# The second routing done batch by batch inside the last attention's loop, with fixed slots per expert

## What is computed

```python
x = x + xattn0(layernorm(x), ctx, ...)      # 16 heads of 32, causal
x = x + ffn0(layernorm(x), ...)             # 8 experts, top 2, gelu, 512 -> 2048 -> 512
x = x + xattn1(layernorm(x), ctx, ...)      # 16 heads of 64; keys and values: own rows and 722 context rows
x = x + ffn1(layernorm(x), ...)             # 8 experts, top 2, silu(gate)*up, 512 -> 1024 -> 512

# ffn1:
logits = einsum('bsd,ed->bse', x, w_router)
top_vals, top_idx = top_k(logits, 2); rw = softmax(top_vals)
h = silu(x @ w_gate[e].T) * (x @ w_up[e].T); y = h @ w_down[e].T   # for the two experts of each row
out = layernorm(sum(rw * y of the chosen experts)) * ln_gamma + ln_beta
```

## Time and profile before

| | us |
|---|---|
| median of 3 runs | 1887.82 |
| profiled execution | 1884.81 |
| its span, first to last instruction | 1883.2 |
| TensorE busy | 1651.2 (88%) |
| VectorE busy | 1075.2 (57%) |
| ScalarE busy | 769.7 (41%) |
| POOL busy | 135.2 (7%) |

### The profile page before, as it was taken

One profiled execution on the slowest core, in us unless ns is written; L12 is line 12 of the kernel. 1 busy time (PEld: TensorE's weight loads), 2 busy tenths in 40 slices (PEclk: granted clock), 3 DMA queues, 4 the chain that ended last, 5 costly groups with the idle time before them and its releaser, 6 DMA issues. The chain is left out here.

```text
span 1883.2 us, 31881 instructions
## 1 busy us (share of the span) xinstructions
PE 1651.2 (88%) x11680; PEld 1399.7 (74%) x11680; DVE 1075.2 (57%) x1776; ACT 769.7 (41%) x1464; POOL 135.2 (7%) x177
## 2 busy tenths in 40 slices
PE   6997359999999779989999899899998619999993
PEld 5785349999999469668787687678777519999981
DVE  5775547677666552246556365456555327767765
ACT  2453135555555232235444254435444015445440
POOL 4000320000000300200000000000000040000004
PEclk9998569999999889989999899999999659999997
DMA  9300165665566434231110101111000065555634
GB/s 345 138 9 1 60 235 203 204 212 206 200 204 210 130 132 148 86 119 33 31 44 23 46 17 46 34 30 41 22 17 9 1 226 197 207 210 192 218 135 125
DMA packets 83938, 223.51 MB, mean 119 GB/s; under 512 B 32904, under 2 KB 39432, under 8 KB 68748
## 3 DMA queue, kind: packets, MB, share of 16 engines
q1 hardware_dynamic: 68412, 175.72, 28.0%
q0 software_dynamic: 15440, 46.56, 7.1%
HBM read 180.61 MB, written 41.62 MB: 118 GB/s over the span
## 5 line engine op out<-in xcount | busy, mean ns | idle before, releaser
L955 DVE TENSOR_TENSOR e_lo<-e_raw,e_hi 128x2048 fp32r<-128x2048 f32 x118 | 270.4, 2291 | 129.0 <-ACT e_hi L1018 129.0
L918 PE MATMUL banks<-e_xh,e_hi 128*128 128x256 f32 x1024 | 292.1, 285 | 12.3 <-DVE e_xl L971 7.4
L1564 PE MATMUL banks<-a_ch,a_wm 128*128 128x362 f32 (+1 forms) x1024 | 286.0, 341 | 10.4 <-DVE a_cl L1680 10.4
L918 PE MATMUL banks<-e_xl,e_hi 128*128 128x256 f32 x1024 | 291.4, 285 | 0.0
L918 PE MATMUL banks<-e_xh,e_lo 128*128 128x256 f32 x1024 | 291.4, 285 | 0.0
L1018 ACT CAST e_hi<-e_raw 128x2048 fp32r<-128x2048 f32 x118 | 224.7, 1904 | 70.5 <-PE banks L935 28.6
L918 PEld LDWEIGHTS banks<-e_xh,e_hi 128*128 128x128 f32 x1024 | 197.6, 193 | 20.7 <-issue 8.2
L918 PEld LDWEIGHTS banks<-e_xl,e_hi 128*128 128x128 f32 x1024 | 197.7, 193 | 5.6
L918 PEld LDWEIGHTS banks<-e_xh,e_lo 128*128 128x128 f32 x1024 | 197.6, 193 | 0.0
L1564 PEld LDWEIGHTS banks<-a_ch,a_wm 128*128 128x128 f32 x1024 | 186.6, 191 | 12.3 <-DVE a_cl L1680 11.8
L1693 DVE TENSOR_REDUCE a_nmax<-banks 100x1 f32<-100x822 f32 x128 | 123.5, 1006 | 107.8 <-PE banks L1598 107.8
(11 more groups left out here) (236 smaller groups left out, 2690.7 us busy)
## 6 DMA issues: line engine op xcount, KB each, us to landing
e_raw<-wout SPq DMA_DIRECT2D x50, 1024.0 KB, 4.8
e_raw<-w SPq DMA_DIRECT2D x34, 1024.0 KB
e_raw<-wgate SPq DMA_DIRECT2D x17, 1024.0 KB
e_raw<-wup SPq DMA_DIRECT2D x17, 1024.0 KB, 4.9
a_craw<-ctxT SPq DMA_DIRECT2D x32, 361.0 KB, 3.8
e_xs<-slot_rows SPq DMA_DIRECT2D x18, 512.0 KB
slot_outs<-e_y POOLq DMA_DIRECT2D x16, 512.0 KB, 3.2
slot_rows<-a_zero POOLq DMA_DIRECT2D x15, 512.0 KB, 10.4
```

The source lines that it names most:

```text
L918: mm = nc.tensor.matmul(ps[:, bank, 0:CAP], w[:, cc, cut], x[:, cc, :], start=t == 0, stop=t == len(terms) - 1)
L955: nc.vector.tensor_tensor(lo[g % 2][i][:], raw[q % RAW][:], hi[g % 2][i][:].bitcast(F32), ALU.subtract)\
L1564: mm = nc.tensor.matmul(ps[:, 6 + half, 0:wide], w[:, cc, cut], x[:, cc, start:start + wide], start=cc == 0 and t == 0, stop=cc == DC - 1 ...
```

## The change

- The loop over batches of the last attention is written out: eight batches in a row, no hardware loop.
- Routing 1 has no stage of its own. In each batch the batch before is routed: output in pair 1 (now ahead of the value product), statistics and root in pair 2, rows in pair 3, turn in 4, logits and best expert in 5, second expert in 6, ranks and slot in 7, then two scatters on POOL's queue. The last batch is routed after the loop.
- Each expert has 1024 fixed slots (`SPAN`), so a slot needs only the count so far. A second table `first_row` gives each pass its first slot. The slot buffer for rows is larger (33 x 256 rows in place of 15), with more zeroing at the start; the results of layer 1 have a buffer of their own (8192 rows), which is first filled by four copies of 4 MB inside device memory on POOL's queue, after the scatters of batches 0 to 3.
- During the last batch SP loads three weight chunks of the first expert; two are split in high and low parts into the space of the context weights. It is always expert 0, as each expert now has a pass at least.
- The softmax of the two chosen logits moves to the start of combine 1.
- Turned probabilities have two buffers in place of four, the attention's output one in place of two.

```diff
+SPAN = CAP * -(-B * T // CAP)
...
-        self.rows = nc.dram_tensor("slot_rows", ((PASSES + 1) * CAP, D), F32, kind="Internal").ap()
-        self.outs = nc.dram_tensor("slot_outs", (PASSES * CAP, D), F32, kind="Internal").ap()
+        self.first_row = self.sb(ctx, "first_row", [1, 16], I32)
+        self.best = self.sb(ctx, "best", [T, 2, B])
+        self.rows = nc.dram_tensor("slot_rows", (E * SPAN + CAP, D), F32, kind="Internal").ap()
+        self.outs0 = nc.dram_tensor("slot_outs0", (PASSES * CAP, D), F32, kind="Internal").ap()
+        self.outs1 = nc.dram_tensor("slot_outs1", (E * SPAN, D), F32, kind="Internal").ap()
...
-                for t, n in ((k.rows, PASSES + 1), (k.outs, PASSES)):
+                pool.wait_ge(w_in["o"], 16)
+                for t, n in ((k.rows, E * SPAN // CAP + 1), (k.outs0, PASSES)):
                     for r in range(n):
                         pool.dma_start(t[CAP * r:CAP * (r + 1)].rearrange("(p s) d -> p (s d)", p=128),
                                        zero[:]).then_inc(zeroed, 16)
-                pool.wait_ge(zeroed, 16 * (2 * PASSES + 1))
+                pool.wait_ge(zeroed, 16 * (E * SPAN // CAP + 1 + PASSES))
...
-        raw = [k.sb(c, f"{L}raw{q}", [128, 4, 512]) for q in range(RAW)]
-        hi = [[k.sb(c, f"{L}hi{u}_{n}", [128, 4, 512], F32R) for n in range(CH)] for u in range(2)]
-        lo = [[k.sb(c, f"{L}lo{u}_{n}", [128, 4, 512], F32R) for n in range(CH)] for u in range(2)]
...
+        READY = 0 if ahead1 is None else len(ahead1.hi)
+        raw = [k.sb(c, f"{L}raw{q}", [128, 4, 512]) for q in range(RAW)] if ahead1 is None else ahead1.raw
...
-                n = sp.value_load(last, min_val=LEAST, max_val=PASSES)
+                if ahead1 is not None:
+                    for q in range(CH):
+                        sp.sem_inc(w_in[q], 16)
...
+                def first_row(j):
+                    if ahead1 is None:
+                        return j * CAP
+                    if type(j) is int:
+                        return 0
+                    return sp.value_load(k.first_row[0:1, bass.ds(j, 1)], min_val=0, max_val=E * SPAN)
...
-                first = expert(0)
-                load(0, first, FIRST)
-                sp.wait_ge(scattered, 16 * 2 * B)
-                rows(0)
-                load(0, first, LATE)
+                if ahead1 is None:
+                    n = sp.value_load(last, min_val=LEAST, max_val=PASSES)
+                    first = expert(0)
+                    load(0, first, FIRST)
+                    sp.wait_ge(scattered, 16 * 2 * B)
+                    rows(0)
+                    load(0, first, LATE)
+                else:
+                    rows(0)
+                    n = sp.value_load(last, min_val=LEAST, max_val=PASSES)
...
-                for b in range(B):
+                for b in range(B if ahead1 is None else 0):
...
-                    pool.dma_start(k.outs[bass.ds(j * CAP, CAP), :].rearrange("(s p) d -> p s d", p=128), y[:])\
+                    first = j * CAP if ahead1 is None else \
+                        pool.value_load(k.first_row[0:1, bass.ds(j, 1)], min_val=0, max_val=E * SPAN - CAP)
+                    outs = k.outs0 if ahead1 is None else k.outs1
+                    pool.dma_start(outs[bass.ds(first, CAP), :].rearrange("(s p) d -> p s d", p=128), y[:])\
...
+                    nc.vector.tensor_tensor(sm[:, 0, :], k.best[:, 1, :], k.best[:, 0, :], ALU.subtract).then_inc(dif, 1)
+                    dve.wait_ge(wexp, 1)
+                    own.link(nc.vector.tensor_scalar(sm[:, 1, :], sm[:, 0, :], 1.0, None, ALU.add))
+                    own.link(nc.vector.reciprocal(k.wt[:, 0, :], sm[:, 1, :]))
+                    own.link(nc.vector.tensor_tensor(k.wt[:, 1, :], k.wt[:, 0, :], sm[:, 0, :], ALU.mult))
...
+                    act.wait_ge(dif, 1)
+                    nc.scalar.activation(sm[:, 0, :], sm[:, 0, :], ACT.Exp).then_inc(wexp, 1)
...
+    def __init__(self, k, ctx, s1):
+        self.names = ["wgate", "wup", "wout1"]
+        self.raw = [k.sb(ctx, f"e1_raw{q}", [128, 4, 512]) for q in range(3)]
+        self.hi = [s1.wm[0][:, :, 512 * i:512 * i + 512] for i in range(2)]
+        self.lo = [s1.wm[1][:, :, 512 * i:512 * i + 512] for i in range(2)]
+
...
-    OUTPUT_AT = 1
+    OUTPUT_AT, STATS_AT, ROWS_AT, TURN_AT, LOGITS_AT, SECOND_AT, RANK_AT = 1, 2, 3, 4, 5, 6, 7
...
+    CLEAR = 4
+    CLEAR_ROWS = E * SPAN // CLEAR
...
-        PT = [k.sb(c, f"a1_PT{u}", [128, len(KB1), T]) for u in range(4)]
-        yT = [k.sb(c, f"a1_yT{u}", [128, IC, T]) for u in range(2)]
+        PT = [k.sb(c, f"a1_PT{u}", [128, len(KB1), T]) for u in range(2)]
+        yT = k.sb(c, "a1_yT", [128, IC, T])
...
         def over_steps(eng, step):
 
-            def batch(b, u):
+            for b in range(B):
                 for m in range(IC):
-                    step(b, u, m)
-
-            batch(0, 0)
-            with eng.Fori(0, (B - 2) // 2) as i:
-                batch(2 * i + 1, 1)
-                batch(2 * i + 2, 0)
-            batch(B - 1, 1)
+                    step(b, b % 2, m)
...
+                    if b == B - 1 and m < len(ahead1.raw):
+                        sp.dma_start(ahead1.raw[m][:], a[ahead1.names[m]][0]).then_inc(raw_in[m], 16)
...
+                sp.wait_ge(raw_in[len(ahead1.raw) - 1], 16)
...
+                for b in range(B):
+                    pool.wait_ge(va, b + 1)
+                    pool.tensor_tensor(rs[:, b:b + 1], rs[:, b:b + 1], k.nhalf[:, 0:1], ALU.pow).then_inc(rstd, 1)
+                    pool.wait_ge(slotted, b + 1)
+                    for j in range(2):
+                        pool.indirect_dma_start(out=k.rows[:, :],
+                                                out_offset=bass.IndirectOffsetOnAxis(ap=k.slot[:, j, b:b + 1], axis=0),
+                                                in_=rows[b % 2][:], in_offset=None).then_inc(scattered[b % 2], 16)
+                    if b < CLEAR:
+                        part = slice(CLEAR_ROWS * b, CLEAR_ROWS * (b + 1))
+                        pool.dma_start(k.outs1[part].rearrange("(p s) d -> p (s d)", p=128),
+                                       k.outs0[0:CLEAR_ROWS].rearrange("(p s) d -> p (s d)", p=128))\
+                            .then_inc(cleared, 16)
+                pool.wait_ge(cleared, 16 * CLEAR)
+                for u in range(2):
+                    pool.wait_ge(scattered[u], 16 * B)
...
-                def output(b, u):
+                def keys_copied(b, m):
+
+                    if exists(IC * b + m + 2):
+                        pe.wait_ge(k_v, IC * b + m + 3)
+
+                def output(b):
 
                     pe.wait_ge(ys, IC * (b + 1))
-                    if later(b):
-                        pe.wait_ge(k_v, IC * (b + 1) + OUTPUT_AT + 3)
+                    keys_copied(b + 1, OUTPUT_AT)
...
+
+                def route_turn(b):
+                    pe.wait_ge(rn, b + 1)
+                    keys_copied(b + 1, TURN_AT)
+                    for cc in range(DC):
+                        mm = nc.tensor.transpose(ps[:, 7, T * cc:T * cc + T], rows[b % 2][:, 128 * cc:128 * cc + 128],
+                                                 k.ident[0:T, 0:T])
+                    mm.then_inc(rt, 1)
+
+                def route_logits(b):
+                    pe.wait_ge(rx, b + 1)
+                    if b == 0:
+                        pe.wait_ge(w_in, 16)
+                    keys_copied(b + 1, LOGITS_AT)
+                    for cc in range(DC):
+                        mm = nc.tensor.matmul(ps[0:T, 7, 0:E], rxT[:, cc, :], wg[:, cc, :],
+                                              start=cc == 0, stop=cc == DC - 1)
+                    mm.then_inc(lg, 1)
+
+                def route_rank(b):
+                    pe.wait_ge(sel_r, b + 1)
+                    if b == 0:
+                        pe.wait_ge(made_more, 1)
+                    keys_copied(b + 1, RANK_AT)
+                    nc.tensor.matmul(ps[0:T, 7, 0:E], upper[:], sel[:], start=True, stop=True)
+                    nc.tensor.matmul(ps[0:T, 7, E:2 * E], ones[:], sel[:], start=True, stop=True).then_inc(rk, 1)
...
+                    if m == TURN_AT + 1:
+                        after(pe, rx, b)
+                    if m == LOGITS_AT + 1:
+                        after(pe, lgc, b)
+                    if m == (RANK_AT + 1) % IC:
+                        after(pe, rkc, b - 1)
                     memory_ahead(b, u, m, 1)
                     if exists(p + 1):
                         turn_values(p + 1, (m + 1) % IC)
+                    if m == OUTPUT_AT and b >= 1:
+                        output(b - 1)
                     if prev:
                         attended(p - 1, *back(b, m))
-                    if m == OUTPUT_AT and exists(p - IC):
-                        output(b - 1, 1 - u)
+                    if m == TURN_AT and b >= 1:
+                        route_turn(b - 1)
+                    if m == LOGITS_AT and b >= 1:
```

(95 more changed lines are left out.)

133 lines of the change are left out of this document (114 added, 19 removed).

## The result

Over four runs each, the changed kernel takes 1835.88 us in the median (1834.92 to 1839.31) and the kernel before 1887.53 us. The ratio is 0.9738, with a 95% interval of 0.9726 to 0.9749: 2.6% faster. The forecast was 1833 us, in a range of 1823 to 1852. The profiled execution took 1834.92 us and its span is 1833.3 us, against 1884.81 and 1883.2 before.

A forecast was written before the change was run, and what follows sets the result against it. TensorE was taken as nearly always busy in the last attention and mostly idle from there to the experts. Span 1883.2 - 21.1 + 11.3 - 43.3 = 1830.1, execution 1831.7, median put at 1833 us, range 1823 to 1852.

The forecast's parts named there:

- Part 1: Last attention's loop written out straight: the two loop jumps go, -21.1 us, or 0 if the wait came with the address.
- Part 2: Routing of batches 0 to 6 inside the last attention's loop: 1.6 us per batch on TensorE, +11.3 us, bounds +8 to +28.
- the room of 0.85 us: Pair 5 of the loop: from the end of the turned probabilities' copy to the values' turn; maxima about 0.7 us late.
- -9.8: Forecast shift in us of the last statistics at the attention's end, against 1478.11 before.
- Part 3: DMAs moved (weight loads, 4 MB copies, more zeroing stores): taken as 0, upper bounds +32 us for copies, +6 for zeroing.
- Part 4: End of last attention to first expert matmul: 25.3 us in place of 68.6, -43.3 us, bounds -38 and -46.
- Part 5: Softmax weights moved into the last stage: about 2.7 us, covered by the first product's 14.37 us gather wait, taken as 0.
- the case without cover: Last stage: the moved softmax not hidden behind the gather wait, costing 2.7 us.
- A: Rival: loop insertions stall TensorE on late copies in four pairs per batch, 14 to 28 us, 1847 to 1861; chance 0.13.
- C: Rival: added stores and copies hold up loads, up to 38 us, 1871, more likely 1845; chance 0.07.
- B: Rival: the wait at the loop jump stays as block changes of a longer program, 1854 us; chance 0.04.
- D: Rival: instruction fetch lags straight-line code, 10.5 us per refill, slower from 6 refills, 1917 at one per batch; chance 0.04.

## Why the prediction was right

**Part 1, -21.1.** Right in mechanism and size: the loop alone written out gives -21.1 us on the timeline and -20.6 us between medians. One reading behind it was wrong without effect: batches outside the loop do show waits on the instruction stream, two of 2.9 us together in the last batch, and they stayed.

**Part 2, +1.6 per batch.** The mechanism was right, shown by the doubled logits. The term was under-sized: 1.85 us, 7 x 0.25 = 1.8 us in all. Turns 0.50 for 0.45, logits 0.80 for 0.67, ranks 0.45 for 0.5. Logits at full clock were taken as half of what they cost at half clock in a row of 64. A row of eight takes more: 0.80 us to the start of what follows. In the doubled run the second eight added 0.71 us, near the 0.67, so most of the difference comes once with each group. The remaining 0.1 us of the 1.85 has no row of its own. No wait showed at pairs 1, 4, 5 and 7, so the room of 0.85 us that was read off sufficed.

**The last batch**, which the sum took as moving with the others, cost more. From the seventh projection to the last it is 71.72 us, against 67.46 in the written-out kernel before. Of these 4.26 us, 1.85 are the routing and 1.2 come back that the first projection had gained (it goes ahead of the value product in the loop, 85.55 us behind the first scores in place of 86.75, but not in the last batch). Some 1.2 us are left that no run explains. The splits of the weights are not the cause: without them it is 71.64 us. The last output projection took 8.95 us in place of 7.91. Windows of the changed kernel (busy us of PE, PEld, DVE, ACT, POOL with counts, clock, DMA share, GB/s) show the clock:

```profile
1450.00:1455.00 5.00, 4.01 (x26) 3.14 (x23) 0.71 (x5) 1.05 (x3) 2.03 (x2) 0.50 0.11 28
1455.00:1459.00 4.00, 2.63 (x29) 2.32 (x28) 3.15 (x3) 0.18 (x2) 0.00 (x0) 0.50 0.22 68
1459.00:1464.00 5.00, 4.88 (x7) 1.88 (x8) 2.29 (x1) 1.86 (x2) 0.00 (x0) 0.62 0.00 0
```

TensorE, idle some of the time as the last pairs run out, stands at the lower of its two levels (1.2 GHz) from 1450 and is granted 2.4 GHz again only within the projection. In the kernel before it had come back sooner in that product. But the length of this product is spread between executions and no price of the change: in the second profiled execution of the changed kernel the product took 7.41 us, with a granted clock of 0.93 in the 5 us from 1461, in which it began, where the row above has 0.62. Against all this the stage began 1.4 us sooner: the first scores, which wait for the load of the output bias in the kernel before, start at 819.68 in place of 821.12. With the loop only written out they start at 820.05, and in the second execution of the changed kernel at 821.84, so this too is spread between executions and no gain of the change.

So -9.8 became -7.9: +1.8 in the loop, +1.2 and +1.0 in the last batch, -1.4 at the start, and -0.5 as the last batch is shorter when written out (67.46 us in place of 67.98). These make -7.7.

**Part 3, 0.** Right. The copies, priced alone, are worth nothing, and neither 47 nor 79 stores made the first attention longer.

**Part 4, -43.3.** Right to 0.7 us. The chain to the slot took 8.5 us for 8.9 (end of statistics 1470.24, slots 1478.73). From the slots to SP's DMA of the rows it is 8.8 us for 5.0 + 2.5 = 7.5: the two scatters 2.7 for 2.5, then 6.1 us for landing, the stage change and the first address together, where 2.5 + 2.5 was taken. This term was under-sized by 1.1 us. Rows to first matmul took 8.8 us for 8.9. The two scatters beside the pass table took 1.04 and 0.99 us, no longer than elsewhere, so the bound that was held open for them was not used.

**Part 5, 0.** The failing step. It was argued from the wait of TensorE for the first gather, which is indeed as long (13.31 us for 14.37). But what sets the end there is the sequence of sixteen gathers on GpSimd, and what the softmax moved was not work ahead of TensorE but how VectorE's additions meet that sequence, later and without a pause ahead of them: 24.5 us from the first gather's start to the last one's end, in place of 21.7. Work that is put under a cover has to be followed further: what it delays on its own engine can meet the other engines at another place. Its price was 2.9 us from the first gather to the end. For the case without cover 2.7 had been named, by another mechanism; that the two are close is luck. Ahead of it the way from the last expert's store to the first gather was 1.3 us shorter (7.12 us before, also with the loop alone written out, and 5.8 us in all kernels with the new stages), a difference that no run here explains. The expert passes, from the first matmul to the last store, were 1.0 us shorter. So the table shows only +0.6: that the miss of this part hardly shows in the total is luck.

By the Trainium skill ("SBUF — State Buffer", section "SBUF: two separate sides") VectorE and GpSimd share a pair of ports by an exclusive lock that is held for a whole instruction. It names two kinds of VectorE instruction that take it: those in a mode that uses two ports, beside which a DMA issued from GpSimd can't get its descriptors written, and those with two inputs in SBUF, against a GpSimd operation that reads SBUF. By that rule the trace agrees that a gather is held to the end of VectorE's work and not slowed in proportion: 4.84 and 5.79 us, ended 0.87 and 0.86 us behind the additions. It differs in two things, and the measurement decides. The additions are of the second kind, for which the section infers that descriptors can still be written, and yet they held gathers up; whether they met the gather's reading of its slots from SBUF, no run shows. And a gather waited not for one addition of 0.68 us but for up to eight in a row. The section also doesn't say why the same eight cost 1.0 us in all in the kernel before.

**The rivals.** A and C were put at 0.13 and 0.07 and are shown to be empty; B and D at 0.04 each fall with the loop written out alone. The span came out 3.2 us above the sum: 1.9 in the attention, 0.7 between the stages and 0.6 behind them. The median lies 1.0 us above the profiled execution; the forecast had allowed some 1.5.

## What to carry to other kernels

Where one engine has no gap, price an insertion by starts, from its own start to the start of what follows, at the clock that holds there: this was good to 0.1 us a batch. Here the routing of a batch, done inside such a loop, cost little more than its matmuls (1.75 of 1.85 us), and all the rest of it left the stage boundary. Before moving VectorE work near a run of gathers or scatters on GpSimd, look at what else it shifts: long elementwise work on VectorE belongs where no indirect DMA is being issued, here in the wait for the first rows, worth 4.3 us.

## What the runs showed of the hardware

A gather issued by GpSimd took 0.98 to 1.17 us when VectorE was idle or did 100x100 products from one source tile. Nine profiles have the eight back-to-back additions of 100x512 in fp32 beside the gathers. In six of them one gather took 4.8 us or more: 4.84 to 4.85 us in the two executions of the changed kernel and in the three kernels that leave the last stage as it is, and 5.79 us in the kernel with the ten products. In the other three (the kernel before, the same with its loop written out, the early softmax) two gathers took 1.5 us and none stood still, but the second of them also ended 0.85 to 0.86 us behind the additions (1852.40 against 1851.54 in the kernel before).

What sorts the nine is the pause ahead of the additions: VectorE was idle for 0.40, 0.50 and 0.57 us in the three, waiting for the offset's load, and not at all in the six. The moment sorts them less simply: the additions start 0.12, 0.23 and 0.29 us behind the start of a gather in the three, but 0.40 us in five of the six and 0.04 us in the sixth. No run changes the one without the other, so the cause stays open.

A jump of the loop cost 10.2 and 10.9 us between output projections, of which 7.6 and 8.8 us are idle time of TensorE; written out, the same kernel showed no wait on the instruction stream up to the last batch.
